# Message layer of a graph network: worked transposed, features spread over the partitions by fp32 matmuls

## The chip, the core and the metric

The program runs on one core of a Trainium2 chip. The metric is the device time of one execution in microseconds (us). The engines are TensorE (PE), VectorE (DVE), ScalarE (ACT), GpSimd (POOL) and the sync engine (SP); each works off its own list in order, and they wait for each other on semaphores. SBUF has 128 partitions; PSUM, where matmuls write, has eight banks of 512 fp32 a partition.

## The reference

Two message-passing layers on 12,500 nodes of 32 features and 200,000 edges, each followed by x = layernorm(x + aggregate). The edges come sorted by target node. Layer 0 takes the mean of the source features per target. Layer 1, the message layer, computes one 32-feature message per edge from the source's features, the edge's weight d and its direction r, and sums them per target:

```python
R = jax.nn.relu(d[:, None] @ w1 + b1) @ w2 + b2          # (E, 384)
Y = spherical_harmonics(rel_vec)                           # (E, 9)
Fj = features[src]                                         # (E, 32): 8 scalars, 8 vectors of 3
for i, (mo, lo) in enumerate(RS):                          # RS = [(8, 0), (8, 1)]
    for j, (mi, li) in enumerate(RS):
        for k, lf in enumerate(range(abs(lo - li), lo + li + 1)):
            acc += _NORM[i] * einsum('euv,ef,evi,ofi->euo', Rb[..., k], Yf, Fb, C)
```

The kernel rotates the vectors of an edge into a frame along r. There the message is, for every edge, a product of 384 radial values R with features and a sum over the 8 input channels v, for 32 outputs (8 scalars u and 3 components of 8 vectors u); then it rotates back.

## The kernel before, in words

Each partition holds 1564 consecutive edges, one edge per column. Columns are worked in batches of T = 16 (98 batches; the last has TL = 12), two batches k = 0, 1 per loop round. The message layer is the function layer1 of every engine. A batch there goes through these steps:

- POOL (lines 653-665): 16 indirect DMAs gather one source row of 32 features for each partition, one DMA per column, into got[k]; it may refill got[k] when rotated_in and f0_copied say that batch b-2 is read.
- SP (line 509): loads hid[k] (edge weights, copied to 64 partitions twice: even columns on partitions 0-63, odd ones on 64-127), the frames, and stores finished runs. It waits for radial_ready of an earlier batch.
- ACT (lines 786-809): relu turns the weights into the hidden layer; further the copies of the scalars (line 800), two of the turned components (803, 804), masks (700) and the turning of runs for the store (704).
- DVE (lines 1560-1605): rotation into the frame (1570 to 1581), then, for 6 groups of 3 or 2 columns (SIZES), two products of PSUM radial values with features (1592 and 1600) and a halving (1547) of the sum over v from 16 to 8 terms; in between turn_back (1534) of batch b-2 and its segmented scan (1350, 1355).
- PE (lines 966-992): radial(b, k, g) gives for each column of a group one bias matmul in bf16 (961) and one fp32 matmul (963), stationary hid (64 rows, 128 edges), moving wc (384 columns), into ps_r with edges on partitions. add_halves (934) sums the 8 remaining terms by 8 matmuls with the identity, add_axes (951) the three rotated-back components. PE's order is written out by hand in layer1; DVE's as well.

After the stage the node stage (L642, L1483 and on) gathers the sums of each node and normalises.

## Time and profile before

| | us |
|---|---|
| median of 3 runs | 3832.39 (3831.2 to 3833.62) |
| span of the profiled execution | 3826.4 |
| median less that span | 6.0 |
| PE busy | 3266.5 (85%) |
| DVE busy | 3211.4 (84%) |
| POOL busy | 2845.1 (74%) |
| ACT busy | 1391.8 (36%) |

The profile shows one execution; its own time is given as its span, from the first to the last instruction, and the runs' times are taken outside it. Busy times are shares of the whole span, with layer 0 in the first 1450 us and the message layer from about 1600 to 3690 us. A matmul in fp32 shows as two records. PEclk is the TensorE clock that was granted, as a share of 2.4 GHz.

### The profile page before, as it was taken

To read this page: it belongs to the slowest core of one execution; us is meant where nothing else is said; L and a number is where in the kernel's file an instruction comes from. 1 tells how busy PE (TensorE), PEld (TensorE's weight loads), DVE (VectorE), ACT (ScalarE), POOL (GpSimd) and SP (SyncE) were. 2 spreads that over 40 slices of the span, in tenths; PEclk is the share of its full clock that TensorE was granted. 3 is DMA by queue.
4 is the path that set the end of the run, shared out by engine and by line. 5 is a ranking of instruction groups with operands and counts; after the bars stand their busy time and mean duration, and the time that the engine had idled before them with its cause. 6 is when DMAs were issued, how large, how long until landed. Compare 5 with 4: busy or idle time off the path is not lost. (4 is left out here: it accounts for less than half of the span.)

```text
span 3826.4 us, 51167 instructions
## 1 busy us (share of the span) xinstructions
PE 3266.5 (85%) x14783; PEld 2108.0 (55%) x14783; DVE 3211.4 (84%) x4450; ACT 1391.8 (36%) x1803; POOL 2845.1 (74%) x2915
## 2 busy tenths in 40 slices
PE   4999999999999883288888988988989889889873
PEld 3898889898989773233333433333433334334342
DVE  5787877787878784589999999999999999999975
ACT  3777777776777650011111111111111111111110
POOL 7777777777777776677777777777777777777746
PEclk9999999999999995599999999999999999999985
DMA  4122222222222221122222222222222222222211
GB/s 99 39 56 41 54 40 43 52 45 50 44 52 41 50 51 27 37 54 54 61 52 57 56 61 52 60 52 60 53 61 51 61 51 61 52 61 55 58 33 25
DMA packets 188426, 197.62 MB, mean 52 GB/s; under 512 B 60241, under 2 KB 149427, under 8 KB 188085
## 3 DMA queue, kind: packets, MB, share of 16 engines
q1 hardware_dynamic: 95508, 149.13, 13.4%
q0 software_dynamic: 92832, 47.72, 10.1%
q14 instruction: 77, 0.63, 0.1%
q8 instruction: 9, 0.15, 0.0%
HBM read 134.02 MB, written 62.59 MB: 51 GB/s over the span
## 5 line engine op out<-in xcount | busy, mean ns | idle before, releaser
L663 POOL DMA_INDIRECT got<-x_d,idx x1564 | 1562.3, 999 | 510.0 <-issue 501.9
L963 PE MATMUL ps_r<-wc,hid 64*128 64x384 f32 x3128 | 791.4, 485 | 0.0
L886 PE MATMUL ps_r<-x_hi,hot_s 128*128 128x448 f32 x1974 | 742.7, 376 | 41.6 <-ACT hot_s L717 41.6
L886 PE MATMUL ps_r<-x_lo,hot_s 128*128 128x448 f32 x1974 | 733.5, 372 | 0.0
L704 ACT COPY runs_t<-runs 128x512 f32<-128x512 f32 x196 | 211.7, 1080 | 1098.8 <-DVE runs L1355 1098.7
L1592 DVE TENSOR_TENSOR prod<-ps_r,f_along 128x768 f32<-128x768 f32 (+1 forms) x586 | 503.3, 859 | 61.2 <-PE ps_r L963 31.4
L714 ACT ACTIVATE hot_s<-rows,minus_row 128x512 fp32r<-128x512 f16 (+1 forms) x658 | 448.9, 763 | 245.1 <-PE ps_m L886 204.7
L1600 DVE TENSOR_TENSOR prod<-ps_r,f_across 128x768 f32<-128x768 f32 (+1 forms) x586 | 504.2, 860 | 0.0
L963 PEld LDWEIGHTS ps_r<-wc,hid 64*128 64x128 f32 x3128 | 421.0, 190 | 106.7 <-issue 1.6
L934 PE MATMUL ps_m<-x_room,ident 128*128 128x512 f32 x768 | 409.6, 659 | 69.3 <-DVE x_room L1547 69.3
L934 PE MATMUL ps_m<-unit,ident 128*128 128x512 f32 x784 | 401.7, 637 | 48.6 <-DVE unit L1547 48.6
L886 PEld LDWEIGHTS ps_r<-x_hi,hot_s 128*128 128x128 f32 x1974 | 378.6, 192 | 75.8 <-issue 42.9
L886 PEld LDWEIGHTS ps_r<-x_lo,hot_s 128*128 128x128 f32 x1974 | 378.6, 192 | 33.0
L617 POOL DMA_INDIRECT got<-in_x_dram,idx_deep x322 | 312.3, 970 | 107.8 <-issue 43.2
L617 POOL DMA_INDIRECT f_across<-in_x_dram,idx_deep x331 | 314.7, 951 | 100.9 <-issue 43.0
L617 POOL DMA_INDIRECT f_along<-in_x_dram,idx_deep x326 | 315.4, 967 | 99.3 <-PE ps_r L886 40.2
L961 PE MATMUL ps_r<-bias_parts,ones_b 64*128 64x384 bf16 x1564 | 262.8, 332 | 132.7 <-DVE prod L1600 110.6
L886 PE MATMUL ps_m<-x_hi,hot_s 128*128 128x448 f32 x987 | 362.0, 367 | 0.0
L886 PE MATMUL ps_m<-x_lo,hot_s 128*128 128x448 f32 x987 | 361.5, 366 | 0.0
L961 PEld LDWEIGHTS ps_r<-bias_parts,ones_b 64*128 64x128 bf16 x1564 | 62.6, 93 | 526.5 <-DVE prod L1600 331.3
L717 ACT ACTIVATE hot_s<-hot_s 128x3584 fp32r<-128x3584 f32 x94 | 336.1, 3576 | 3.0
L934 PEld LDWEIGHTS ps_m<-x_room,ident 128*128 128x128 f32 x768 | 139.8, 202 | 283.0 <-issue 278.7
(202 smaller groups left out, 4427.9 us busy)
## 6 DMA issues: line engine op xcount, KB each, us to landing
hid<-weight_t SPq DMA_DIRECT2D x196, 256.0 KB
run_d<-runs_t SPq DMA_DIRECT2D x194, 256.0 KB
got<-x_d,idx POOLq DMA_INDIRECT x1564
rows<-code_d SPq DMA_DIRECT2D x47, 160.0 KB, 3.4
frame_d<-x_sb SPq DMA_DIRECT2D x7, 1008.0 KB, 4.5
frame<-frame_d SPq DMA_DIRECT2D x98, 72.0 KB
frame_b<-frame_d SPq DMA_DIRECT2D x98, 72.0 KB, 1.9
rows<-code_d SPq DMA_DIRECT2D x47, 128.0 KB
```

The costliest lines, as they stand in the source:

```text
L617: pool.indirect_dma_start(got_deep[k][:, t, :], None, x, bass.IndirectOffsetOnAxis(ap=idx_deep[q][:, k * T + t:k * T + t + 1], axis=0)).th ...
L663: pool.indirect_dma_start(got[k][:, t, :], None, x1_d, bass.IndirectOffsetOnAxis(ap=idx[k][:, t:t + 1], axis=0)).then_inc(got2_landed[k], 16)
L704: act.copy(runs_t[k][:, :, :], runs[k][:, :, :].rearrange("p f t -> p t f")).then_inc(done, 1)
L714: act.activation(hot_s[k][:, a, :, :], rows[k][:, :, :], ACT.Abs, bias=minus_row[:, a:a + 1]).then_inc(off_rows, 1)
L717: act.activation(hot_s[k][:, :, :, :], hot_s[k][:, :, :, :].bitcast(F32), ACT.Relu, bias=1.0, scale=-1.0).then_inc(hot_s_ready, 1)
L886: mm = pe.matmul(found[BANK_OF[k][g]], hot_s[k][:, a, g, :], part[:, a * LN * D:(a + 1) * LN * D], start=(a == 0 and n == 0), stop=(a == B ...
L934: mm = pe.matmul(terms2[k].rearrange("p o t -> p t o"), ident[:, :], halves[k][:, v, :, :], start=(v == 0), stop=(v == MUL - 1))
L961: pe.matmul(ps_r[:, g % 2, t, 0:RD], ones_b[rows, :], bias_parts[rows, :], start=True, stop=False)
L963: pe.matmul(ps_r[:, g % 2, t, 0:RD], hid[k][rows, c * P:(c + 1) * P], wc[rows, :], start=False, stop=True).then_inc(radial_ready, 1)
L1592: dve.tensor_tensor(prod[q][:, 0:size, 0:2, :, :], ps_r[:, q, 0:size, 0:256].rearrange("p t (b v u) -> p t b v u", b=2, u=MUL), spread(f_a ...
L1600: dve.tensor_tensor(prod[q][:, 0:size, 2:4, :, :], spread(ps_r[:, q, 0:size, 256:RD].rearrange("p t (v u) -> p t v u", u=MUL), 2, 2), spre ...
```

## The change

A batch is worked with (column, feature) on the partitions and edges along the free dimension.

- PE: `radial` now has wc stationary (128 of its 384 columns) and hid moving: a unit (c, h) gives 128 radial values for 4 x 128 edges of two columns-in-four, as two matmuls of 64 rows by 512 columns into the two banks of the one `radial_slot`. ACT copies each unit to SBUF and adds the bias there (`copy_radial`); the six bias matmul groups go. `turn_features` transposes the rotated features (4 transposes), ACT copies them to `ft`, and `spread_features` repeats them over 128 partitions by a matmul of 32 rows by 512 columns with a 0/1 matrix, two per unit, into two alternating slots of two banks.
- DVE: `multiply` makes 8 products of 2 x 512 elements per batch (SBUF times PSUM into SBUF). There is no halving.
- PE: `sum_products` sums over v by a matmul with a 0/1 matrix of 32 columns, 4 matmuls (one per column-in-four, each to 32 partitions of the one bank `summed_p`) for each of 4 blocks q. ACT copies the sums (`copy_summed`), `turn_messages` transposes them back (4 transposes), and from there turn_back, add_axes and the scan go as before, but for batch b-1 instead of b-2 and with one PSUM bank, so the scalars are copied out and added back by one more matmul.
- hot_p's room is used again for radial copies; the bias split in bf16 parts goes; a bias column and the 0/1 matrices are made at the start of the stage.

The core of the diff:

```diff
+            def copy_radial(b, u, w=QUAD * P):
+                c, h = RADIAL_UNITS[u]
+                act.wait_ge(radial_ready, UNITS * b + u + 1)
+                if not isinstance(b, int) or b > 0:
+                    act.wait_ge(multiplied, len(PRODUCTS) * (b - 1) + (1, 2, 3, 4, 7, 8)[u])
+                act.activation(radial_s[u][:, :, 0:w], radial_slot[:, :, 0:w], ACT.Identity,
+                               bias=bias_col[:, c:c + 1]).then_inc(radial_copied, 1)
+            def copy_summed(b, w=QUAD * P):
+                act.wait_ge(summed, BLOCKS * (b + 1))
+                if not isinstance(b, int) or b > 0:
+                    act.wait_ge(messages_ready, b)
+                act.copy(summed_t[:, 0:w], summed_p[:, 0:w]).then_inc(summed_copied, 1)
...
+                    first, final = isinstance(b, int) and b == 0, last and k == 1
+                    n = TL if final else T
+                    w = TL // QUAD * P if final else QUAD * P
+                    if not first:
+                        copy_summed(b - 1)
                     act.wait_ge(got2_landed[k], 16 * (T * i + n))
                     if not isinstance(b, int) or b > 1:
+                        act.wait_ge(turned, b - 1)
+                    act.copy(turned_in[k][:, 0:n, 0:MUL], got[k][:, 0:n, 0:MUL]).then_inc(f0_copied, 1)
+                    copy_radial(b, UNITS - 1, w)
                     act.copy(idx[k][:, :], src_all[:, bass.ds((b + 2) * T, T)]).then_inc(idx_ready, 1)
+                    act.wait_ge(turned, b + 1)
+                    if not first:
+                        act.wait_ge(spread_ready, UNITS * b)
+                    act.copy(ft[:, 0:w], spread_slot[k][:, 0, 0:w]).then_inc(ft_ready, 1)
+                    if not first:
+                        masks2(b - 1, 1 - k)
+                    if not final:
+                        later = TL // QUAD * P if last else QUAD * P
+                        for u in range(4):
+                            copy_radial(b + 1, u, later)
+                    if not first:
+                        carry_and_turn(b - 1, 1 - k)
+                    if not last:
+                        relu(k, i + 2)
+                    if not final:
+                        copy_radial(b + 1, 4, later)
...
+            def radial(b, k, u, w=QUAD * P):
+                c, h = RADIAL_UNITS[u]
+                if u == 0:
+                    pe.wait_ge(hid_ready, b + 1)
+                if not isinstance(b, int) or UNITS * b + u > 0:
+                    pe.wait_ge(radial_copied, UNITS * b + u)
+                for t in range(2):
+                    half = slice(t * H, (t + 1) * H)
+                    mm = pe.matmul(radial_slot[:, t, 0:w], wc[half, c * P:(c + 1) * P],
+                                   hid[k][half, :].rearrange("p (j c e) -> p j c e", c=2, e=P)[:, 0:w // P, h, :],
+                                   start=True, stop=True)
+                mm.then_inc(radial_ready, 1)
+            def turn_features(b, k, w=QUAD * P):
+                pe.wait_ge(rotated_in, b + 1)
+                pe.wait_ge(f0_copied, b + 1)
+                if not isinstance(b, int) or b > 0:
+                    pe.wait_ge(multiplied, len(PRODUCTS) * b - 1)
+                for j in range(w // P):
+                    mm = pe.transpose(spread_slot[k][:, 0, j * P:(j + 1) * P],
+                                      turned_in[k][:, QUAD * j:QUAD * (j + 1), :].rearrange("p t f -> p (t f)"), ident[:, :])
+                mm.then_inc(turned, 1)
+            def spread_features(b, k, s, w=QUAD * P):
+                c, h = SPREADS[s]
+                slot = spread_slot[(k + s + 1) % 2]
+                if s == 0:
+                    pe.wait_ge(ft_ready, b + 1)
+                    if not isinstance(b, int) or b > 0:
+                        pe.wait_ge(multiplied, len(PRODUCTS) * b)
+                if s > 1:
+                    pe.wait_ge(multiplied, len(PRODUCTS) * b + (2, 4, 5, 6)[s - 2])
+                for t in range(2):
+                    group = slice((2 * h + t) * D, (2 * h + t + 1) * D)
+                    mm = pe.matmul(slot[:, t, 0:w], repeat[group, c, :], ft[group, 0:w], start=True, stop=True)
+                mm.then_inc(spread_ready, 1)
+            def sum_products(b, q, w=QUAD * P):
+                pe.wait_ge(multiplied, len(PRODUCTS) * b + (3, 4, 6, 8)[q])
+                if q == 0 and (not isinstance(b, int) or b > 0):
+                    pe.wait_ge(summed_copied, b)
+                for t in range(QUAD):
+                    mm = pe.matmul(summed_p[t * D:(t + 1) * D, 0:w], to_feature[:, D - MUL - q * MUL:2 * D - MUL - q * MUL],
+                                   product[q][t // 2][:, t % 2, 0:w], start=(q == 0), stop=(q == BLOCKS - 1))
+                mm.then_inc(summed, 1)
+            def turn_messages(b, w=QUAD * P):
+                pe.wait_ge(summed_copied, b + 1)
+                if not isinstance(b, int) or b > 0:
+                    pe.wait_ge(scanned, BATCHES + b)
+                for j in range(w // P):
+                    mm = pe.transpose(ps_m[:, 0, j * P:(j + 1) * P], summed_t[:, j * P:(j + 1) * P], ident[:, :])
+                mm.then_inc(messages_ready, 1)
...
             def layer1(i, last=False):
                 for k in range(2):
                     b = 2 * i + k
+                    first, final = isinstance(b, int) and b == 0, last and k == 1
+                    short = TL // QUAD * P
+                    w = short if final else QUAD * P
+                    later = short if last else QUAD * P
+                    if not first:
+                        sum_products(b - 1, 3)
+                        turn_messages(b - 1)
+                    turn_features(b, k, w)
+                    if not final:
+                        radial(b + 1, 1 - k, 0, later)
+                    spread_features(b, k, 0, w)
+                    spread_features(b, k, 1, w)
+                    if not first:
+                        add_axes(b - 1)
+                    if not final:
+                        radial(b + 1, 1 - k, 1, later)
+                    spread_features(b, k, 2, w)
+                    sum_products(b, 0, w)
+                    sum_products(b, 1, w)
+                    if not final:
+                        radial(b + 1, 1 - k, 2, later)
+                    spread_features(b, k, 3, w)
+                    if not final:
+                        radial(b + 1, 1 - k, 3, later)
+                    spread_features(b, k, 4, w)
+                    if not final:
+                        radial(b + 1, 1 - k, 4, later)
+                    spread_features(b, k, 5, w)
+                    sum_products(b, 2, w)
+                    if not final:
+                        radial(b + 1, 1 - k, 5, later)
...
+            def multiply(b, k, n, w):
+                q, h = PRODUCTS[n]
+                u = RADIAL_UNITS.index((min(q, 2), h))
+                s_ = SPREADS.index((max(q - 1, 0), h))
+                dve.wait_ge(radial_copied, UNITS * b + u + 1)
+                dve.wait_ge(spread_ready, UNITS * b + s_ + 1)
+                if h == 0 and (not isinstance(b, int) or b > 0):
+                    dve.wait_ge(summed, BLOCKS * (b - 1) + q + 1)
+                dve.tensor_tensor(product[q][h][:, :, 0:w], radial_s[u][:, :, 0:w], spread_slot[(k + s_ + 1) % 2][:, :, 0:w],
+                                  ALU.mult).then_inc(multiplied, 1)
             def layer1(i, first, last=False):
                 for k in range(2):
                     b = 2 * i + k
                     short = last and k == 1
                     n = TL if short else T
+                    w = n // QUAD * P
                     dve.wait_ge(got2_landed[k], 16 * (T * i + n))
                     dve.wait_ge(frame_loaded[k], 16 * (i + 1))
...
                     for c in range(3):
                         s.mark(dve.tensor_tensor(part[:, c, 0:n], spread(f1[:, :, :, c], 2, 3),
                                                  spread(frame[k][:, 0:n, c, :], 3, MUL), ALU.mult))
+                    s.settle()
+                    s.mark(dve.tensor_tensor(part[:, 0, 0:n], part[:, 0, 0:n], part[:, 1, 0:n], ALU.add))
+                    s.settle()
+                    if not isinstance(b, int) or b > 1:
+                        dve.wait_ge(turned, b - 1)
+                    dve.tensor_tensor(turned_in[k][:, 0:n, MUL:D], part[:, 0, 0:n].rearrange("p t i v -> p t (i v)"),
+                                      part[:, 2, 0:n].rearrange("p t i v -> p t (i v)"), ALU.add).then_inc(rotated_in, 1)
                     if not (first and k == 0):
+                        turn_back(b - 1, 1 - k)
+                    for m in range(4):
+                        multiply(b, k, m, w)
+                    if not (first and k == 0):
+                        scan2(b - 1, 1 - k)
+                    for m in range(4, len(PRODUCTS)):
+                        multiply(b, k, m, w)
```

## Rows read from the trace of the kernel before

**Rows 1.** Stretches: stretch, length; busy us of PE, PEld, DVE, ACT, POOL; PEclk, DMA, GB/s
```profile
1700.00:3600.00 1900.00, 1700.35 (x6285) 751.42 (x6285) 1789.19 (x2605) 330.41 (x626) 1436.10 (x1438) 0.97 0.25 57
```
**Rows 2.** The page: granted TensorE clock in 40 equal slices of the span
```profile
PEclk9999999999999995599999999999999999999985
```
**Rows 3.** Instructions of line 1570: durations, first and last start
```profile
L1570 DVE TENSOR_TENSOR part<-got,frame x294: 532/665/687, 1615.3 to 3665.9; 128x384 f32<-128x384 f32 x146, 128x288 f32<-128x288 f32 x1
```
**Rows 4.** Groups by line, shapes apart, 1700 to 3600 us
```profile
L663 POOL DMA_INDIRECT got<-x_d,idx x1438 | 1436.8, 999 | 464.1 <-issue 464.1
L963 PE MATMUL ps_r<-wc,hid 64*128 64x384 f32 x2871 | 722.7, 482 | 0.0
L934 PE MATMUL ps_m<-x_room,ident 128*128 128x512 f32 x720 | 384.2, 659 | 65.6 <-DVE x_room L1547 65.6
...
L1592 DVE TENSOR_TENSOR prod<-ps_r,f_along 128x768 f32<-128x768 f32 x360 | 342.3, 951 | 55.0 <-DVE f_across L1581 27.2 <-PE ps_r L963 26.5
...
L951 PE MATMUL ps_m<-back,ident 128*128 128x384 f32 x540 | 190.2, 489 | 0.0
...
L1570 DVE TENSOR_TENSOR part<-got,frame 128x384 f32<-128x384 f32 x270 | 164.7, 665 | 49.7 <-DMA got<-x_d,idx 49.0
L1534 DVE TENSOR_TENSOR back<-ps_m,frame_b 128x384 f32<-128x384 f32 x270 | 133.7, 554 | 0.0
...
L788 ACT ACTIVATE hid<-hid,b_col,w_col 128x1024 f32<-128x1024 f32 x90 | 110.3, 1225 | 0.0
...
L704 ACT COPY runs_t<-runs 128x512 f32<-128x512 f32 x89 | 96.7, 1086 | 899.5 <-DVE runs L1355 899.5
...
L700 ACT COPY masks<-same 128x480 f32 x89 | 52.6, 591 | 0.0
L1577 DVE TENSOR_TENSOR part<-part 128x384 f32<-128x384 f32 x90 | 49.8, 553 | 0.0
```
**Rows 5.** Waits, 1700 to 3600 us: who for whom, us, times, longest
```profile
ACT f_along L800 <- DMA got<-x_d,idx: 144.7, 57, 6.1
...
DVE part L1570 <- DMA got<-x_d,idx: 49.0, 24, 3.8
```
**Rows 6.** Instructions of line 663, 1700 to 3600 us
```profile
L663 POOL DMA_INDIRECT got<-x_d,idx x1438: 940/944/1692, 1700.1 to 3599.7; - x180
```
**Rows 7.** Timeline of DVE: start, length, instruction
```profile
3000.85 0.95 DVE L1592 TENSOR_TENSOR prod<-ps_r,f_along 128x768 f32<-128x768 f32 x1
3001.72 0.95 DVE L1547 TENSOR_TENSOR x_room<-prod 128x768 f32<-128x768 f32 x1
...
3012.13 0.68 DVE L1592 TENSOR_TENSOR prod<-ps_r,f_along 128x512 f32<-128x512 f32 x1
3012.73 0.68 DVE L1547 TENSOR_TENSOR x_room<-prod 128x512 f32<-128x512 f32 x1
```
**Rows 8.** Timeline of PE, one batch (a matmul in fp32 is two records)
```profile
3002.71 1.12 PE L934 MATMUL ps_m<-unit,ident 128*128 128x512 f32 x2
...
3005.48 1.98 PE L934 MATMUL ps_m<-unit,ident 128*128 128x512 f32 x4
...
3006.88 0.59 PE L934 MATMUL ps_m<-unit,ident 128*128 128x512 f32 x1
...
3007.57 0.81 PE L963 MATMUL ps_r<-wc,hid 64*128 64x384 f32 x4
3008.31 0.70 PE L934 MATMUL ps_m<-unit,ident 128*128 128x512 f32 x1
```
**Rows 9.** Instructions of line 859, fp32 transposes of layer 0
```profile
L859 PE MATMUL ps_r<-ident,prod_room x4: 421/421/477, 41.4 to 42.1; 128*128 128x128 f32 x3, 128*39 128x128 f32 x1
```
**Rows 10.** Timeline of DVE, end of the message layer
```profile
3681.53 0.95 DVE L1600 TENSOR_TENSOR prod<-ps_r,f_across 128x768 f32<-128x768 f32 x1
...
3690.07 1.22 DVE L1355 TENSOR_TENSOR_SCAN runs<-masks,ps_m 128x512 f32<-128x512 f32 x1
```
**Rows 11.** Timelines of PE and ACT, start of the message layer
```profile
1601.38 0.80 PE L961 MATMUL ps_r<-bias_parts,ones_b 64*128 64x384 bf16 x3 [18.30 <-DVE bias_parts L1266]
...
1615.31 0.40 ACT L800 COPY f_along<-got 128x256 f32<-128x256 f32 x1 [15.56 <-DMA got<-x_d,idx]
```

More of the change, by code:

```diff
@@ L28 @@
 NPP = 98
-SG = 3
-SIZES = (3, 3, 3, 3, 2, 2)
-GROUPS = len(SIZES)
-FIRST = [sum(SIZES[:g]) for g in range(GROUPS)]
+QUAD = 4
+HALVES = 2
+BLOCKS = 4
+RADIAL_UNITS = ((0, 0), (1, 0), (0, 1), (1, 1), (2, 0), (2, 1))
+PRODUCTS = ((0, 0), (1, 0), (0, 1), (1, 1), (2, 0), (2, 1), (3, 0), (3, 1))
+SPREADS = ((0, 0), (0, 1), (1, 0), (1, 1), (2, 0), (2, 1))
+UNITS = len(RADIAL_UNITS)
 NC = 7
@@ L673, in _ @@
             pool.wait_ge(ngot_used[0], CHUNKS)
-            pool.wait_ge(radial_ready, T * (BATCHES - 1) + TL)
+            pool.wait_ge(radial_ready, UNITS * BATCHES)
             pool.sem_inc(pool_go, 1)
@@ L803, in layer1 @@
-                    act.copy(f_across[k][:, 0:n, 1, 0, :], f_across[k][:, 0:n, 0, 1, :]).then_inc(turned_copied, 1)
-                    act.activation(f_across[k][:, 0:n, 1, 1, :], f_across[k][:, 0:n, 0, 0, :], ACT.Copy,
-                                   scale=-1.0).then_inc(turned_copied, 1)
-                    if not (last and k == 1):
-                        relu(1 - k, i + 1 + k)
-                    if not isinstance(b, int) or b > 1:
-                        carry_and_turn(b - 2, k)
+                    act.wait_ge(turned, b + 1)
@@ L953, in add_axes @@
-                mm.then_inc(axes_summed, 1)
-            def radial(b, k, g):
-                if not isinstance(b, int) or b > 0 or g > 1:
-                    pe.wait_ge(multiplied, GROUPS * b + g - 1)
-                tiles = [((FIRST[g] + t) // 2, slice((FIRST[g] + t) % 2 * H, (FIRST[g] + t) % 2 * H + H))
-                         for t in range(SIZES[g])]
-                for t, (c, rows) in enumerate(tiles):
-                    pe.matmul(ps_r[:, g % 2, t, 0:RD], ones_b[rows, :], bias_parts[rows, :], start=True, stop=False)
-                for t, (c, rows) in enumerate(tiles):
-                    pe.matmul(ps_r[:, g % 2, t, 0:RD], hid[k][rows, c * P:(c + 1) * P], wc[rows, :],
-                              start=False, stop=True).then_inc(radial_ready, 1)
+                    pe.matmul(terms2[:, MUL:D, :].rearrange("p (u i) t -> p t i u", i=3)[:, 0:n], ident[:, :],
+                              back[:, a, 0:n], start=(a == 0), stop=(a == 2), skip_group_check=True)
@@ L997, in _ @@
+            pe.wait_ge(wc_ready, 1)
+            pe.wait_ge(bias_made, 1)
+            for c in range(3):
+                mm = pe.transpose(turned_bias[:, c * P:(c + 1) * P], bias_rooms[1][:, c * P:(c + 1) * P], ident[:, :])
+            mm.then_inc(bias_turned, 1)
+            for u in range(UNITS):
+                radial(0, 0, u)
+            pe.wait_ge(bias_ready, 1)
+            pe.wait_ge(spreads_made, 1)
             layer1(0)
@@ L1241, in make_wc, with make_constants @@
                                                 ALU.mult, ALU.add)
-            def make_bias_parts():
-                b2_all, bias, left, part_f = bias_rooms
-                for n in range(3):
-                    s.mark(dve.tensor_scalar(part_row[:, n:n + 1], node[:, 0:1], float(NPP * n), None, ALU.is_equal))
-                s.mark(dve.memset(ones_b[:, :], 1.0))
+            def make_constants():
+                b2_all, bias = bias_rooms
                 dve.wait_ge(loaded_b2, 16)
+                last = make_wc(b2_all, bias)
+                last.then_inc(bias_made, 1)
+                s.mark(dve.memset(to_feature[:, :], 0.0))
+                s.mark(dve.tensor_reduce(in_group[:, :], ident[:, :].rearrange("p (t f) -> p f t", f=D), AX.X, ALU.add))
@@ L1250, in make_bias_parts @@
                 s.settle()
-                for n in range(3):
-                    s.mark(dve.scalar_tensor_tensor(part_row[:, n:n + 1], node[:, 0:1], float(NPP * (H + n)),
-                                                    part_row[:, n:n + 1], ALU.is_equal, ALU.add))
-                s.mark(make_wc(b2_all, bias))
-                s.settle()
-                s.mark(dve.tensor_copy(bias_parts[:, :], bias))
-                s.settle()
-                s.mark(dve.tensor_tensor(left, bias, bias_parts[:, :], ALU.subtract))
@@ L1571, in layer1 @@
                                                  spread(frame[k][:, 0:n, c, :], 3, MUL), ALU.mult))
-                    if not (first and k == 0):
-                        halve(b - 1, 1 - k, GROUPS - 1)
-                    if not first:
-                        turn_back(b - 2, k)
                     s.settle()
@@ L1607, in _ @@
+                    if not (first and k == 0):
+                        scan2(b - 1, 1 - k)
+                    for m in range(4, len(PRODUCTS)):
+                        multiply(b, k, m, w)
             loop(layer1, PAIRS - 1, 2)
             layer1(PAIRS - 1, False, True)
-            halve(BATCHES - 1, 1, GROUPS_L - 1)
-            turn_back(BATCHES - 2, 0)
-            turn_back(BATCHES - 1, 1, part, False, TL)
-            for b in (BATCHES - 2, BATCHES - 1):
-                scan2(b, b % 2)
+            turn_back(BATCHES - 1, 1, TL)
```

193 lines of the change are left out of this document (66 added, 127 removed).

## The prediction, written before the changed kernel was run

> **What bounds the kernel now.** I read the table of stretches first. From 1700 to 3600 us the message layer runs in steady state: DVE is busy for 1789 of 1900 us, PE for 1700, ACT for only 330, at a granted clock of 0.97 of 2.4 GHz [rows 1]. The gaps in that clock are short: the slices show 9 nearly everywhere but at the two node stages [rows 2]. The first and last start of line 1570, three per batch, give the length of a batch: (3665.9 - 1615.3) / 97 = 21.1 us [rows 3]. Anything saved or lost per batch counts 98 times.
>
> By that table DVE looks like the bound. The groups by line show a second one. POOL issues one gather per column: 1438 of them, 1436.8 us busy and 464.1 us between them, which is 1.32 us each and 1901 us of 1900 [rows 4]. Sixteen make 21.1 us, exactly the batch. The idle time is all "issue", the fixed 0.3 us that follows each gather; POOL waits for almost nobody. The other side of it is in the waits: DVE's line 1570 waited 49.0 us and ACT's line 800 144.7 us for gathered rows [rows 5]. So two engines are at their limit together, and POOL is untouched by the change. Its gathers take 0.944 us at the median, 0.94 at least and 1.69 at most [rows 6]; if all took 0.94 a batch would still need 16 x (0.94 + 0.305) = 19.9 us. **No relief of DVE can bring more than 21.1 - 19.9 = 1.2 us per batch, 118 us in all**; what gathers lose beyond 0.944 us has to go too for that.
>
> **The change part by part.** Per batch of 16 columns, with durations from the steady state.
>
> *DVE.* Removed are 12 products and 6 halvings. One 768-element operation starts 0.87 us after the other (3000.85, 3001.72), one of 512 elements 0.60 us (3012.13, 3012.73) [rows 7]. There are 12 of the large and 6 of the small: 14.0 us. Added are 8 products of 1024 elements. The two rows lie on a line of 0.27 us per 256 elements, so 1.14 us each, 9.1 us. Line 1579 and 1581 together become one 384-element operation (0.55 us as line 1577 [rows 4]); a 128-element copy ahead of turn_back adds about 0.2. DVE's own sum, with busy time of a line over 90 batches: parts 164.7/90 = 1.8, add 0.6, rotated 0.55, copy 0.2, turn_back 133.7/90 = 1.5, products 9.1, carry and scan 1.5 [rows 4]: **15.2 us**. It stops being a bound.
>
> *ACT.* Added: 6 bias copies of 1024 elements out of PSUM, 1 of 512 for the sums, 1 of 512 for the turned features. Line 788 does 1024 elements in 1.225 us, line 700 480 in 0.59 [rows 4]. A copy from PSUM has no row at this size; between as fast as line 788 and half as much again. I take line 788's. New ACT sum: 6 x 1.2 + 2 x 0.65 + masks 0.6 + turned runs 1.1 + ReLU 1.2 + small ones 0.4 = 11.8 us. It fits, but in written order: the copies of radial unit 4 stand behind turned runs and the ReLU.
>
> *PE.* Removed: 16 bias matmuls in bf16, 16 of 384 columns, 8 sums of halves of 512 columns. Added: 12 radial and 12 spreading matmuls of 512 columns, 16 summing ones of 512 columns by 32, 8 transposes, and one 128-column matmul beside the axes. An fp32 matmul of 512 columns shows as two records; between two of them line 934 goes on at 0.86 us (1.98 us for four records, 1.12 for two [rows 8]). What 40 such matmuls cost depends on how many run side by side: one after another they are 34 us. For row halves the trace answers: the four records of line 963 at 3007.57 are two matmuls on partitions 0-63 and 64-127, each record 0.48 us long, and all end 0.81 us later [rows 8]; one alone would take 0.86 x 384/512 = 0.64 and a tail of about 0.17. So **two row groups in different banks run wholly side by side**: a pair of 512 columns costs 0.86 us. The radial pairs are of this kind; the spreading pairs are on 32 rows instead of 64, and I take the same. 12 pairs: 10.3 us (20.6 if nothing overlapped).
>
> The 16 summing matmuls use all 128 rows and four different column groups, all in one bank. **No row before shows column groups.** Side by side, four cost 0.86 us and a batch 3.4 us; in sequence 13.7 us; in twos 6.9. I take 3.4, since row groups overlap fully, and keep the others as cases. The Trainium skill, "TensorE: Matmul & The Clock Gate", Part 3, reports a speed-up of 2.38 for three column tiles of 512 columns; as an estimate from that ratio, a three-tile group costs 3/2.38 = 1.26 of one matmul, so a sum of four about 1.1 us instead of 0.86. The total by that page would be near 3990 us, by full overlap 3890, and no run here shows it yet.
>
> Axes: three full-height matmuls of 384 columns, as now, are 3 x 0.86 x 384/512 = 1.9, and the one of 128 columns 0.2. Transposes: four lines 859 start within 0.7 us, 0.23 each, near the start of the kernel [rows 9]; half that if only the clock differs. 8 x 0.16 = 1.3 us.
>
> A change of shape has a price as well. After the pair at 3007.57 the next full-height matmul starts at 3008.31, 0.74 us later instead of 0.64, and then takes 0.70 us where its neighbours take 0.59 [rows 8]: 0.2 us, its weights not loaded ahead. The new order of PE changes shape 16 times a batch (now 8 times). That is 3.2 us, or 1.6 where weights of 32 columns load fast.
>
> PE's sum: 10.3 + 3.4 + 2.1 + 1.3 + 3.2 = **20.3 us** (18.7 with the cheap shape changes, 19.4 if the first two spreads, on four row groups, overlap). Now it is 1700 / 90 = 18.9.
>
> *New waits on PE.* PE takes its waits in written order, and two of them cover nothing. First, after the last sum of a batch it waits for ACT's copy of the sums before it can turn the messages: tail 0.17, copy 0.65, two handoffs of 0.05 = 0.9 us. Behind it are queued turn_features and everything DVE needs for its next product. Second, radial results have a single slot; unit u+1 waits until ACT has copied unit u: 0.17 + 1.2 + 0.1 = 1.5 us after its end, of which a spreading pair and a shape change hide 1.1. That leaves about 0.4 us three times when the copies are prompt. The last of them (unit 5) waits for the copy of unit 4, and that waits for DVE's seventh product. But the DVE products need the spreads only just made, so part of these waits run while DVE catches up and the summing matmuls would have waited too. I take 0.9 + 0.6 = 1.5 us. **PE's round: 21.8 us**; bounds 20.3 (waits covered, cheap shapes) to 22.8.
>
> *What moves.* SP's reload of hid waits for radial_ready of batch b-1, which now comes a batch earlier; POOL's gathers still wait for rotated_in and f0_copied, both early in a batch. hid is reloaded before it is needed: a round is left for it. A batch is finished one round earlier (b-1 instead of b-2), which changes only the end. There the last product at 3681.53 and the last scan at 3690.07 [rows 10] are 8.5 us apart; new: sum 0.8, copy 0.65, transposes 0.7, turn_back 1.4, axes 1.6, carry and scan 1.5, handoffs 0.4 = 7 us: -1.5. In front, PE starts at 1601.38 and ACT's first copy of gathered features at 1615.31 [rows 11]; six radial units with copies at 2.4 us each fit in these 14 us. Then the first product comes some 3 us later. Together +1 us, nothing.
>
> *Sum.* 21.8 - 21.1 = +0.7 us x 98 = +69 us. With small change at start and end the span goes from 3826.4 to about 3896. The median of the runs shown, 3832.4, lies 6.0 above that span; rounding down for the overlap that the first two spreads may have, I say **3890 us**.
>
> **The rivals.**
> 1. *Column groups run one after another.* For it: no row shows them, and all four stream 128 rows at once, unlike the row halves. Against it: the row halves overlap without any loss. Price: sums 13.7 instead of 3.4, 10.3 us per batch, of which the waits absorb about 0.9: 31.2 us, +10.1 x 98 = +990, **4820 us**.
> 2. *They overlap only partly* (two at a time, or slowed by the shared bank). Sums 5 to 7 us: round 23.5 to 25.3, **4060 to 4240 us**.
> 3. *The gathers bind and PE fits under them: faster.* Place: PE's round. Price and turning point: shape changes at 0.1 us and all waits covered give 18.7 + 0.9 = 19.6, under POOL's 21.1; it decides below 21.0. If the gathers stretch less beside a DVE with 6 us of rest, the batch falls to 20.0-20.9: -0.2 to -1.1 us, **3725 to 3813 us**. For it: gathers of 0.944 us are the median and the stretched ones come in bursts. Against: the 256 KB loads of hid per half, which stay, run in the same bursts.
> 4. *The same with gathers as slow as now:* the batch stays 21.1, **3832 us**.
>
> **How the numbers follow.** Forecast (round 21.3 to 23.2, 3845 to 4040): 0.39. Rival 1: 0.14. Rival 2: 0.14. Rival 3: 0.25. Rival 4: 0.08. A measurement of this kernel tells 0.2%, 8 us, from no change. Faster 0.25, same 0.08, slower 0.67. The forecast's own range is 3845 to 4040; the range for 8 in 10 has to take in rivals 3 and 2, so 3750 to 4350, leaving out rival 1 and the best twentieth of rival 3.
>
> **What would show it.** DVE busy per batch near 15 us, with idle time ended by spreads. Pairs on 32 rows: four records within about 1.05 us. The summing matmuls: eight records within about 1.1 us if side by side, 3.5 if not; this one group tells forecast from rival 1. PE busy over 90% of the stage and POOL no longer 100%: idle behind rotated_in. If POOL still is at 16 x 1.32 us with no waits, the forecast was wrong and rivals 3 or 4 hold. ACT copies of 1024 from PSUM much above 1.3 us would move the bound to the chain through the single radial slot.

## The result, and the profile after

The changed kernel takes 3801.41 us (3798.03 to 3805.39) against 3833.01: a ratio of 0.9921, 95% interval 0.9909 to 0.9932. It is 0.8% faster, 32 us. The forecast was 3890 and slower.

The stretches of the changed kernel, columns as in [rows 1]; first the node stage and the start, then the steady state of the message layer:

```profile
1460.00:1580.00 120.00, 43.57 (x192) 41.71 (x192) 59.67 (x148) 3.89 (x13) 89.78 (x96) 0.50 0.13 25
1580.00:1700.00 120.00, 90.73 (x393) 28.30 (x393) 67.93 (x113) 49.05 (x59) 85.34 (x90) 0.81 0.26 55
1700.00:3600.00 1900.00, 1757.98 (x8736) 574.99 (x8732) 1398.01 (x1729) 958.67 (x1183) 1408.43 (x1463) 1.00 0.26 57
```

Beside [rows 1], DVE fell from 1789 to 1398 us, ACT rose from 330 to 959, PE from 1700 to 1758, and the clock granted to PE is 1.00, where it was 0.97. The gathers are 1463 instead of 1438 in the same time: 1.7% more. The groups by line, which answer to [rows 4]:

```profile
L688 POOL DMA_INDIRECT got<-x_d,idx x1463 | 1409.3, 963 | 491.9 <-issue 474.8 <-ACT f_along L842 17.1
L990 PE MATMUL ps_r<-hid,wc 64*128 64x512 f32 x2184 | 616.4, 641 | 67.4 <-ACT prod_room L822 62.5 <-issue 4.8
L1018 PE MATMUL ps_r<-ft,repeat 32*128 32x512 f32 x2184 | 514.0, 640 | 0.0
L1645 DVE TENSOR_TENSOR x_room<-radial_more,ps_r 128x1024 f32<-128x1024 f32 x364 | 442.1, 1215 | 358.0 <-PE ps_r L1018 240.7 <-ACT prod_room L822 117.3
...
L822 ACT ACTIVATE prod_room<-ps_r,bias_col 128x1024 f32<-128x1024 f32 x364 | 405.6, 1114 | 722.7 <-PE ps_r L990 498.0 <-DVE unit L1645 224.8
...
L1027 PE MATMUL ps_m<-x_room,to_feature 128*32 128x512 f32 x1456 | 193.9, 605 | 0.0
...
L1659 DVE TENSOR_TENSOR part<-got,frame 128x384 f32<-128x384 f32 x273 | 169.6, 677 | 0.0
```

Three readings. DVE now waits for PE's spreads and ACT's copies. The gathers were 0.999 us at the mean and are 0.963, with 0.32 us between them as before (464.1/1438 and 474.8/1463, "issue" alone): sixteen of them with these gaps make 21.1 us before and 20.6 after. And DVE's line 1659 (1570 before) no longer waits for gathered rows: the 49.0 us of [rows 5] are gone. POOL even waits a little for others (17.1 us for ACT). So POOL doesn't seem to be the bound any more; experiment 3 tests it.

One round of PE, from the first two spreads of a batch to those of the next (start, length, instruction; in brackets idle time before it):

```profile
2999.84 1.14 PE L1018 MATMUL ps_r<-ft,repeat 32*128 32x512 f32 x8
3000.91 2.20 PE L1043 MATMUL ps_m<-back,ident 128*128 128x384 f32 x6
3002.95 0.39 PE L1045 MATMUL ps_m<-f_across,ident 128*128 128x128 f32 x2
3003.61 1.13 PE L990 MATMUL ps_r<-hid,wc 64*128 64x512 f32 x4 [0.27 <-ACT prod_room L822]
3004.67 1.13 PE L1018 MATMUL ps_r<-ft,repeat 32*128 32x512 f32 x4
3005.72 1.92 PE L1027 MATMUL ps_m<-unit,to_feature 128*32 128x512 f32 x16
3007.58 1.13 PE L990 MATMUL ps_r<-hid,wc 64*128 64x512 f32 x4
3008.64 1.13 PE L1018 MATMUL ps_r<-ft,repeat 32*128 32x512 f32 x4
3010.00 1.13 PE L990 MATMUL ps_r<-hid,wc 64*128 64x512 f32 x4 [0.24 <-ACT prod_room L822]
3011.06 1.13 PE L1018 MATMUL ps_r<-ft,repeat 32*128 32x512 f32 x4
3012.42 1.13 PE L990 MATMUL ps_r<-hid,wc 64*128 64x512 f32 x4 [0.23 <-ACT prod_room L822]
3013.48 1.13 PE L1018 MATMUL ps_r<-ft,repeat 32*128 32x512 f32 x4
3014.54 1.07 PE L1027 MATMUL ps_m<-x_room,to_feature 128*32 128x512 f32 x8
3015.53 1.13 PE L990 MATMUL ps_r<-hid,wc 64*128 64x512 f32 x4
3016.59 1.07 PE L1027 MATMUL ps_m<-x_room,to_feature 128*32 128x512 f32 x8
3018.44 0.65 PE L1037 MATMUL ps_m<-ident,f_across 128*128 128x128 f32 x4 [0.78 <-ACT f_across L829]
3019.05 0.65 PE L1002 MATMUL ps_r<-ident,f_along 128*128 128x128 f32 x4
3019.63 1.13 PE L990 MATMUL ps_r<-hid,wc 64*128 64x512 f32 x4
3020.68 1.14 PE L1018 MATMUL ps_r<-ft,repeat 32*128 32x512 f32 x8
```

PE's round (the time that one batch takes it) is 3020.68 - 2999.84 = 20.84 us. Four waits make 0.27 + 0.24 + 0.23 + 0.78 = 1.52 us of it. A pair of 512 columns with its change of shape is 1.06 us. Four summing matmuls on four column groups (eight records) take 1.07 us. And the first two spreads, four matmuls on four row groups, also take 1.14 us together.

### The profile page after: what moved, and what is told of

Same layout as the page of the kernel before. It is cut to its first block, busy times and chain, and to the rows that moved or that the text cites. A ratio compares the mean times of both kernels' runs of the same rounds, so it can differ in the third digit from the quotient of the medians.

```text
span 3796.3 us, 58108 instructions
## 1 busy us (share of the span) xinstructions
PE 3310.6 (87%) x17312; PEld 1902.1 (50%) x17312; DVE 2762.8 (73%) x3470; ACT 2061.5 (54%) x2391; POOL 2786.3 (73%) x2915
## 4 chain that ended last, share of the span: by engine, by line
PE 70%; ACT 12%; DVE 5%; POOL 5%; issue 5%; DMA 1%; SPq 0%; ACTq 0%; DVEq 0%; POOLq 0%
PE ps_r L940 19%; PE ps_r L990 17%; PE ps_m L1027 10%; PE ps_m L940 10%; PE ps_r L1018 8%; ACT prod_room L822 8%; POOL ngot L667 4%; DVE unit L1645 3%; PE ps_m L1037 2%; PE ps_r L1002 2%; ACT f_across L829 2%; PE ps_r L924 1%; ACT hot_s L739 1%; PE ps_m L1043 1%; ACT hot_s L742 1%
## 5 line engine op out<-in xcount | busy, mean ns | idle before, releaser
L688 POOL DMA_INDIRECT got<-x_d,idx x1564 | 1506.2, 963 | 530.6 <-issue 504.7
L822 ACT ACTIVATE prod_room<-ps_r,bias_col 128x1024 f32<-128x1024 f32 x392 | 435.9, 1112 | 780.0 <-PE ps_r L990 531.9
L1645 DVE TENSOR_TENSOR x_room<-radial_more,ps_r 128x1024 f32<-128x1024 f32 x392 | 475.0, 1212 | 384.0 <-PE ps_r L1018 252.3
L990 PE MATMUL ps_r<-hid,wc 64*128 64x512 f32 (+1 forms) x2352 | 669.8, 646 | 81.2 <-ACT prod_room L822 72.9
L1018 PE MATMUL ps_r<-ft,repeat 32*128 32x512 f32 (+1 forms) x2352 | 553.4, 639 | 1.1 <-ACT ft L848 0.6
L1645 DVE TENSOR_TENSOR unit<-prod_room,ps_r 128x1024 f32<-128x1024 f32 x392 | 451.1, 1213 | 106.9 <-PE ps_r L1018 102.0
L990 PEld LDWEIGHTS ps_r<-hid,wc 64*128 64x128 f32 x2352 | 178.8, 186 | 448.8 <-ACT prod_room L822 255.3
L1018 PEld LDWEIGHTS ps_r<-ft,repeat 32*128 32x128 f32 x2352 | 148.0, 183 | 371.0 <-issue 150.3
L667 POOL DMA_INDIRECT ngot<-run_d,pos x196 | 185.0, 944 | 111.5 <-issue 59.1
L1369 DVE TENSOR_TENSOR prod_room<-ps_r,hot_l 128x448 f32<-128x448 f32 x282 | 167.6, 620 | 118.8 <-PE ps_r L940 109.9
```

Of the source, the lines that this page charges most:

```text
L667: pool.indirect_dma_start(ngot[c][:, j, :], None, table, bass.IndirectOffsetOnAxis(ap=pos[:, node_j:node_j + 1], axis=0)).then_inc(ngot_la ...
L688: pool.indirect_dma_start(got[k][:, t, :], None, x1_d, bass.IndirectOffsetOnAxis(ap=idx[k][:, t:t + 1], axis=0)).then_inc(got2_landed[k], 16)
L822: act.activation(radial_s[u][:, :, 0:w], radial_slot[:, :, 0:w], ACT.Identity, bias=bias_col[:, c:c + 1]).then_inc(radial_copied, 1)
L990: mm = pe.matmul(radial_slot[:, t, 0:w], wc[half, c * P:(c + 1) * P], hid[k][half, :].rearrange("p (j c e) -> p j c e", c=2, e=P)[:, 0:w / ...
L1018: mm = pe.matmul(slot[:, t, 0:w], repeat[group, c, :], ft[group, 0:w], start=True, stop=True)
L1645: dve.tensor_tensor(product[q][h][:, :, 0:w], radial_s[u][:, :, 0:w], spread_slot[(k + s_ + 1) % 2][:, :, 0:w], ALU.mult).then_inc(multipl ...
```

## The experiments

The kernel before ran on the same chip beside each of these runs, at medians of 3829 to 3831 us, and ratios are against it. The changed kernel didn't run again: where a total is set against its 3801.41 us, differences of some 4 us mean nothing. Several of the kernels leave work out or work on wrong data, which is said; they are for timing alone.

**1. Are the first two spreads really side by side, and does PE's round set the time?** The second spread reads the row groups of the first, so its products get the features of other columns.

```diff
-                    group = slice((2 * h + t) * D, (2 * h + t + 1) * D)
+                    g = t if s == 1 else 2 * h + t
+                    group = slice(g * D, (g + 1) * D)
```

> The changed kernel, but the second spread of a batch reads the same two row groups (partitions 0-63) as the first; its products get the features of other columns, nothing else differs. Theory A (PE's written order sets the batch, and the first two spreads run side by side on four row groups): the two spreads take 1.9 us instead of 1.07, the batch 20.83 + 0.85 = 21.7 us, the total 3801 + 83 = about 3885 us. Theory B (the gathers on POOL set the batch and PE has room): POOL's 16 x 1.27 = 20.3 us stay below, the total moves by less than 20 us.

Measured: 3851.04 us (3850.82 to 3854.09), ratio 1.0054 (1.0037 to 1.0071). PE in its steady state:

```profile
3014.18 1.99 PE L1019 MATMUL ps_r<-ft,repeat 32*128 32x512 f32 x8
3016.09 2.20 PE L1044 MATMUL ps_m<-back,ident 128*128 128x384 f32 x6
3018.13 0.39 PE L1046 MATMUL ps_m<-f_across,ident 128*128 128x128 f32 x2
3018.45 1.13 PE L990 MATMUL ps_r<-hid,wc 64*128 64x512 f32 x4
```

The two spreads take 1.99 us instead of 1.14, the 0.85 expected. The total rose by 50 us, 0.51 per batch, not by 83. The last row shows why: the wait of 0.27 us ahead of this radial unit is gone. Work added in front of a wait is paid only beyond it. The total came out 34 us under the 3885 expected. Theory A holds in kind; its price was too high by what the wait absorbs (0.27 of the 0.34 us per batch that are missing; the rest wasn't looked into).

**2. Do column groups run side by side?** Each summing matmul gets 128 stationary columns; the widening of the 0/1 matrix that goes with it is not shown.

```diff
-                    mm = pe.matmul(summed_p[t * D:(t + 1) * D, 0:w], to_feature[:, D - MUL - q * MUL:2 * D - MUL - q * MUL],
-                                   product[q][t // 2][:, t % 2, 0:w], start=(q == 0), stop=(q == BLOCKS - 1))
+                    mm = pe.matmul(summed_p[:, 0:w], to_feature[:, P - MUL - t * D - q * MUL:2 * P - MUL - t * D - q * MUL],
+                                   product[q][t // 2][:, t % 2, 0:w], start=(q == 0 and t == 0),
+                                   stop=(q == BLOCKS - 1 and t == QUAD - 1))
```

> The changed kernel, but each summing matmul has 128 stationary columns (zeros outside its 8) and adds into all 128 partitions, so that there are no column groups; the result is the same. Theory A (column groups run side by side, and without them four matmuls take 4 x 0.86 us): sums cost 13.7 instead of 3.4 us per batch, less some 0.5 us of waits and shape changes that go, so the batch is 30.6 us, the total about 3801 + 98 x 9.8 = 4760 us. Theory B (the side-by-side look of the records is only their model, and the sums are in series already): no change, 3801 us.

Measured: 4817.28 us (4815.58 to 4818.3), ratio 1.2576 (1.2555 to 1.2597): 10.4 us more per batch. The sixteen records of line 1027 that took 1.92 us:

```profile
3006.49 7.13 PE L1027 MATMUL ps_m<-unit,to_feature 128*128 128x512 f32 x16
```

Theory A in kind, though the batch rose by 10.4 us and not by the 9.8 expected (4760 us). This is also the kernel of rival 1 of the prediction, which gave 4820. That it is so near is in part luck: rival 1 started from a round of 21.8 us, which is 0.96 too long, and took off 0.9 us for waits that would absorb a part; nothing like that was absorbed. In the changed kernel, four matmuls on four column groups into one bank show no extra cost: a second group of four adds 1.92 - 1.07 = 0.85 us.

**3 and 4. Which engine bounded the kernel before, and which after?** Both kernels with 12 gathers per batch instead of 16; the other four columns keep old rows. The waits of ACT and DVE for gathered rows count accordingly:

```diff
+GT2 = 12
...
-                    for t in range(TL if last and k == 1 else T):
+                    for t in range(GT2 if rounds > 0 else T):
...
-                    act.wait_ge(got2_landed[k], 16 * (T * i + n))
+                    act.wait_ge(got2_landed[k], 16 * (T + GT2 * i))
```

> The changed kernel, but from the third batch of the message layer on only 12 of the 16 columns are gathered; the other four keep old rows. Theory A (PE binds): 3801 us within 10 us, at best less by what a late gather costs now and then. Theory B (POOL's gathers bind): the batch falls by what they lack, 0.5 us or more, to 3750 us or below.

> The kernel before, with the same cut of the gathers to 12 per batch. Theory A (before, gathers at 1.32 us each set the batch of 21.1 us and DVE alone could do it in 20.25 us, the length of an undisturbed batch in the trace): the total falls by 98 x 0.85 = 83 us to about 3750 us. Theory B (DVE bound it, and the change gained by relieving DVE): 3833 us within 10 us.

Measured: after with 12 gathers 3801.34 us (3796.41 to 3805.9), unchanged; before with 12 gathers 3741.05 us (3740.45 to 3741.7), ratio 0.9767 (0.975 to 0.9783), 90 us less. The gathers of experiment 3 (line 689, 1700 to 3600 us) and then of experiment 4 (line 664, 1700 to 3500 us):

```profile
L689 POOL DMA_INDIRECT got<-x_d,idx x1092 | 1030.4, 944 | 870.4 <-ACT idx L845 558.9 <-issue 311.5
```

```profile
L664 POOL DMA_INDIRECT got<-x_d,idx x1068 | 1064.5, 997 | 735.5 <-issue 735.5
```

So before, the gathers set the batch, and DVE's own round was 21.1 - 90/98 = 20.2 us: with 12 gathers DVE is busy for 1767 of the 1800 us. After, relief of POOL is worth nothing, and experiment 1 showed that added work on PE costs time: PE sets the batch. The rows hold a surprise: a quarter of the gathers is gone in both, but one takes 0.944 us in the first and still 0.997 in the second.

**5. What is next behind PE?** The summing matmuls of blocks 1 and 2 are left out, and with them their share of the messages.

```diff
-                pe.wait_ge(multiplied, len(PRODUCTS) * b + (3, 4, 6, 8)[q])
+                pe.wait_ge(multiplied, len(PRODUCTS) * b + (4, 4, 6, 8)[q])
...
-                mm.then_inc(summed, 1)
+                mm.then_inc(summed, 2)
...
-                    sum_products(b, 1, w)
...
-                    sum_products(b, 2, w)
```

> The changed kernel without the summing matmuls of blocks q = 1 and q = 2 (their share of the messages is left out); PE's batch gets 1.9 us shorter on paper. Theory A (behind PE at 20.83 us the gathers are next, 16 x (0.963 + 0.305) = 20.3 us): the batch stops at 20.3 to 20.4 us, the total near 3755 us. Theory B (nothing but PE is near): 3801 - 98 x 1.5 = 3655 us, a part of the gain being lost in waits for ACT's copies.

Measured: 3759.89 us (3759.65 to 3760.97), ratio 0.9817 (0.9802 to 0.9832). The batch is 20.84 - 41.5/98 = 20.4 us; its gathers are 0.960 us and 0.32 apart, 20.5 for sixteen. Theory A: the gathers stand close behind PE, by 0.4 us in the total of this run, and by 0.2 us in the changed kernel's own rows (20.6 against 20.84).

**6 and 7. PE's longest wait.** In 6 DVE issues line 1659's three products ahead, between its products of the batch before. They become a function `make_part`, and are gone from the start of the batch; shown is where they are issued:

```diff
                     for m in range(4, len(PRODUCTS)):
+                        if m > 4 and not short:
+                            make_part(i + k, 1 - k, m - 5, TL if last else T)
                         multiply(b, k, m, w)
```

In 7, with that, PE and ACT change their order. PE's part is shown; ACT copies `ft` ahead of radial unit 5, and the sums after the indices:

```diff
                         sum_products(b - 1, 3)
-                        turn_messages(b - 1)
                     turn_features(b, k, w)
-                    if not final:
-                        radial(b + 1, 1 - k, 0, later)
+                    if not first:
+                        turn_messages(b - 1)
                     spread_features(b, k, 0, w)
                     spread_features(b, k, 1, w)
+                    if not final:
+                        radial(b + 1, 1 - k, 0, later)
```

> The changed kernel with one edit on DVE: the three rotation products of batch b+1 are issued between the last four products of batch b, where DVE stands idle for 1.1 to 1.5 us each time, instead of after them. Theory A (PE's order and its wait for the copied sums set the batch, and turn_features stands behind turn_messages): no change, 3801 us within 10. Theory B (the rotation on DVE is late and holds PE): the batch gets up to 0.6 us shorter, to about 3745 us.

> As e6, and PE turns the features before it turns the messages, so that this covers its wait of 0.78 us for the copied sums; ACT copies the turned features ahead of radial unit 5, and PE's first radial unit comes after the first two spreads. Theory A (that wait is a real cost of PE's round): PE could do 19.9 us, and the gathers at 16 x 1.27 = 20.3 us take over: total 3801 - 98 x 0.5 = about 3750 us, faster than both kernels. Theory B (another chain, through DVE's turn_back or ACT's single radial slot, is as long): less than 15 us gained.

Measured: 6 gave 3799.31 us (3796.93 to 3800.62), no change, as theory A. But 7 gave 3817.83 (3810.86 to 3822.45), ratio 0.9966 (0.9952 to 0.9979): 16 us slower than the changed kernel, where both theories had it no slower. Excerpts of DVE and POOL of it, where the gathers stretch (the products of line 1646 stand between the DVE rows):

```profile
3002.57 0.67 DVE L1655 TENSOR_TENSOR part<-got,frame 128x384 f32<-128x384 f32 x1 [3.26 <-DMA got<-x_d,idx]
...
3004.28 0.67 DVE L1655 TENSOR_TENSOR part<-got,frame 128x384 f32<-128x384 f32 x1
...
3005.99 0.70 DVE L1655 TENSOR_TENSOR part<-got,frame 128x384 f32<-128x384 f32 x1
...
3007.74 0.55 DVE L1666 TENSOR_TENSOR part<-part 128x384 f32<-128x384 f32 x1
```

```profile
3001.41 0.95 POOL L688 DMA_INDIRECT got<-x_d,idx  x1 [0.30 <-issue]
3002.66 1.38 POOL L688 DMA_INDIRECT got<-x_d,idx  x1 [0.30 <-issue]
3004.34 1.40 POOL L688 DMA_INDIRECT got<-x_d,idx  x1 [0.30 <-issue]
3006.05 1.42 POOL L688 DMA_INDIRECT got<-x_d,idx  x1 [0.30 <-issue]
3007.78 1.33 POOL L688 DMA_INDIRECT got<-x_d,idx  x1 [0.30 <-issue]
3009.41 0.94 POOL L688 DMA_INDIRECT got<-x_d,idx  x1 [0.30 <-issue]
```

Each stretched gather begins while a DVE operation runs whose two inputs are in SBUF. The products of line 1646 in between, with one input in PSUM, stretch none: in the whole steady state 589 gathers began beside one, at 0.944 us in the mean. The first DVE row shows that DVE was waiting for gathered rows again: 7 is bound by gathers, at 0.994 us each, which experiment 8 confirms.

**8. Was PE's round shortened all the same?** As 7, with 12 gathers per batch; the other columns keep old rows.

> As e7, with only 12 of 16 columns gathered from the third batch on (the others keep old rows). Theory A (in e7 the gathers bind at 20.3 us, PE's own round is 19.9 us): about 3715 us, some 35 us under e7. Theory B (e7 is bound by PE or by a chain through ACT or DVE): the same as e7 within 8 us.

Measured: 3707.65 us (3705.65 to 3708.5), ratio 0.968 (0.9665 to 0.9695). PE's round is 20.84 - 93.8/98 = 19.9 us, as worked out. Theory A; the gain is there and the gathers hide it.

**9. The three products in one block**, to touch fewer gathers; the edit is shown against 7:

```diff
-                        if m > 4 and not short:
-                            make_part(i + k, 1 - k, m - 5, TL if last else T)
+                        if m == 6 and not short:
+                            for c in range(3):
+                                make_part(i + k, 1 - k, c, TL if last else T)
```

> As e7 (3818 us, gathers at 0.994 us), but the three rotation products stand in one block ahead of the seventh product instead of singly ahead of the sixth, seventh and eighth. In e7 four gathers in a row took 1.33 to 1.42 us, each beside one of the five spaced DVE operations with two SBUF operands. Theory A (each such operation can hold up one gather, so a block holds up fewer): stretched gathers fall from 2.25 to about 1.5 per batch, the batch from 21.0 to 20.6 us, the total to about 3785 us. Theory B (what counts is only how many such operations there are): as e7, 3818 us.

Measured: 3782.26 us (3780.55 to 3783.74), ratio 0.9874 (0.9858 to 0.9891), the fastest version with the whole work, 19 us under the changed kernel. Gathers:

```profile
L688 POOL DMA_INDIRECT got<-x_d,idx x1469 | 1431.9, 975 | 469.0 <-issue 466.0 <-ACT idx L841 2.1 <-DVE f_along L1670 0.9
```

0.975 + 0.319 = 1.29 us, 20.7 for sixteen: the batch is still POOL's. Theory A: 137 gathers over 1.05 us in 1700 to 3600 us, 1.5 per batch, against 202 and 2.2 in 7, with the same 286 and 287 us of DVE operations on two SBUF inputs.

**10 and 11. Do two SBUF inputs stretch a gather?** Four idle-time products of 512 elements added to the changed kernel, in 10 with the line as shown, in 11 with `ps_m[:, 0, 0:w]` as the second input:

```diff
+                        if m in (5, 6):
+                            for e in range(2):
+                                dve.tensor_tensor(spare_room[:, (2 * (m - 5) + e) * 512:(2 * (m - 5) + e) * 512 + w],
+                                                  radial_s[4][:, 0, 0:w], radial_s[4][:, 1, 0:w], ALU.mult)
```

> The changed kernel with four added DVE products of 512 elements per batch, in the idle time ahead of the sixth and seventh product (two each, 1.2 us, against gaps of 1.5 and 1.3 us); both inputs and the output lie in SBUF, the output is not used. Theory A (a DVE operation with both inputs in SBUF holds up the gathers on POOL): gathers rise from 0.963 us to 1.0 us or more, POOL's batch to 20.9 to 21.3 us, the total to 3815 to 3845 us. Theory B (the stretch has to do with other work at that place, such as the reading of fresh rows): gathers stay at 0.963 us, total 3801 within 10.

> As e10 with one difference: the second input of the four added products is a PSUM bank that is idle then. Theory A (only two SBUF inputs hold up the gathers): gathers 0.963 us, total 3801 within 10. Theory B (any DVE work does, by its share of time): the same rise as e10.

Measured: 10 gave 3818.35 us (3814.8 to 3820.13), ratio 0.9973 (0.9961 to 0.9984); 11 gave 3801.62 (3799.57 to 3805.35), ratio 0.993 (0.9913 to 0.9946), as without the addition. Added products and gathers of 10, then of 11:

```profile
L688 POOL DMA_INDIRECT got<-x_d,idx x1443 | 1439.7, 998 | 461.2 <-issue 457.5 <-ACT f_along L842 3.0 <-ACT idx L844 0.6
...
L1677 DVE TENSOR_TENSOR spare_room<-radial_more 128x512 f32<-128x512 f32 x360 | 231.3, 683 | 0.0
```

```profile
L688 POOL DMA_INDIRECT got<-x_d,idx x1466 | 1412.8, 964 | 489.6 <-issue 472.9 <-ACT f_along L842 16.8
...
L1677 DVE TENSOR_TENSOR spare_room<-radial_more,ps_m 128x512 f32<-128x512 f32 x364 | 232.3, 679 | 0.0
```

The same DVE time, 231 and 232 us. With two SBUF inputs the gathers go from 0.963 to 0.998 us and the total up by 17 us; with one of them in PSUM neither moves. Theory A.

The trace of the kernel before shows the same, gather by gather. Here are a product and a halving of DVE, and two gathers; the halving that the second gather meets, at 3012.73, is in [rows 7]:

```profile
3010.08 0.67 DVE L1592 TENSOR_TENSOR prod<-ps_r,f_along 128x512 f32<-128x512 f32 x1
3010.66 0.95 DVE L1547 TENSOR_TENSOR x_room<-prod 128x768 f32<-128x768 f32 x1
```

```profile
3010.39 0.94 POOL L663 DMA_INDIRECT got<-x_d,idx  x1 [0.30 <-issue]
3012.88 1.34 POOL L663 DMA_INDIRECT got<-x_d,idx  x1 [0.30 <-issue]
```

The first gather begins beside a product that reads PSUM and keeps its 0.94 us, though a halving starts 0.27 us later. The second begins 0.15 us into a halving and ends 0.81 us after it. Over 1700 to 3600 us the 1438 gathers lose 79 us beyond 0.944 each. By the DVE operation that was running as they began, 42 us go to halvings, 30 to line 1570, 7 to line 1581, all with two SBUF inputs; the 682 gathers that began beside a product from PSUM average 0.944 us.

This agrees with a rule of the Trainium skill, "SBUF — State Buffer", section "Who interferes with whom": a DVE operation with two SBUF inputs contends with GpSimd's reads of SBUF, and one with at most one such input does not. The same section of the Trainium skill infers that such a `tensor_tensor` leaves the generation of DMA descriptors alone; here it does hold up the indirect gathers, and the measurement decides.

## Why the prediction was wrong

*What bounds before.* Right: experiment 4 shows the gathers at 21.1 us a batch and DVE at 20.2 behind them. With that the largest possible gain was small, and it was.

*"POOL is untouched by the change."* Wrong, and one of the two steps that failed. The halvings (line 1547, 4.7 us per batch) read two SBUF tiles; the new product reads SBUF and PSUM. With them went 42 of the 79 us by which gathers were stretched, and 28 are left. The mean fell from 0.999 to 0.963 us, and POOL's batch from 21.1 to 16 x (0.963 + 0.325) = 20.6. I had written of this only as a chance in rival 3, as "rest" for DVE. It wasn't rest: experiment 11 gives DVE the same load as 10 and the gathers don't notice. I put the bursts of slow gathers down to the loads of hid; between 10 and 11 those loads are the same and only the place of one DVE operand differs. The floor of 19.9 us was too low as well: it takes 0.305 us between gathers, while [rows 4] have 464.1/1438 = 0.323 at the mean, which makes 20.2.

*PE's round.* Said 21.8, measured 20.84. Its parts:

| term | said | measured |
|---|---|---|
| row pair of 512 columns with its shape change | 0.86 + 0.2 | 1.06 |
| first two spreads | 1.72 | 1.07 with the step to the next |
| summing group of four | 0.86 + change | 1.0 |
| 8 transposes | 1.3 | 1.2 |
| waits | 0.9 + 0.6 | 0.78 + 0.74 |

The mis-sized term is the one of the two spreads, and this is the other step that failed: I took no overlap between them for the central value and named it only as a bound (19.4 instead of 20.3), though they lie on four different row groups and [rows 8] showed that two row groups overlap fully. The runs showed four side by side, 1.07 us for both (experiment 1: 1.99 us without it). That is 0.86 of the 0.96 us, and enough to turn "slower" into "no slower", because the forecast was only 0.7 us above the old batch. It is not enough for "faster": a PE round of 20.9 us under gathers that still take 21.1 is rival 4, 3832 us. For the 32 us that were gained both had to fail, the spreads on PE and POOL's "untouched".

*Column groups.* Right at 3.4 us per batch, without a row for them: four times 0.85, besides the changes of shape. The ratio of 2.38 that the Trainium skill has for three column tiles ("TensorE: Matmul & The Clock Gate", Part 3), from which the prediction estimated 1.1 us for a group of four, isn't borne out here: eight records end within 1.07 us with their tail, and a further group adds 0.85.

*Waits on PE.* Right in place and size (1.5 us). Experiments 1 and 8 show how they count: one absorbed 0.27 of an added 0.85 us, and covering the long one brought the round to 19.9.

*DVE and ACT.* DVE said 15.2 us, measured 1398 / 91 = 15.4. ACT's copy from PSUM said 1.2, measured 1.11. Neither binds, as said.

*The outcome* is rival 3's kind, faster with PE under 21.0, with this difference: the gathers fell below PE, and PE at 20.84 binds. Its range was 3725 to 3813; that 3801 lies in it doesn't make its mechanism right. (Its 19.6 us also adds the wait of 0.9 us that it calls covered.)

*Ends of the stage.* They were taken at nothing, and are worth 8.5 us. From the first and last start of line 1659 (1612.5 and 3641.5 us) the batch is 20.92 us in the mean, against 21.14: 22 of the 30.1 us by which the span is shorter. The others are outside: the first rotation starts 2.8 us earlier, and from the last rotation to the last scan it is 5.7 us less (18.5 against 24.2 us). The mean holds a loss as well: the first batch took 25.2 us, where 20.9 is the median. PE's granted clock was 0.55 from 1596 to 1629 us, and a radial pair took 2.08 us there against 1.13 later.

## What to carry to other kernels

When two engines are at their limit together, a change that relieves one is bounded by the other, and the first test is to cut the other's work; that test, here twelve gathers instead of sixteen, costs a few lines. Look also at which operands of a busy DVE operation lie in SBUF: two SBUF inputs beside a stream of indirect gathers lengthen the gathers, so moving one input to PSUM can speed up POOL without a change on it. And if a forecast hangs on 0.7 us of a 21 us round, an overlap that the rows bear out belongs in the central value, not in the bounds.

## What the runs showed of the hardware

- Four fp32 matmuls on four row groups into four banks, or on four column groups into one bank, take the time of one: 1.14 and 1.07 us for eight records of 512 columns, against 1.12 for one such matmul in [rows 8], 1.99 for two pairs after each other (experiment 1) and 7.13 / 2 = 3.6 us at full width (experiment 2).
- A gather of one row per partition takes 0.944 us alone. If it begins while a DVE operation with two SBUF inputs runs, it can be stretched: to 1.05 to 1.47 us in the changed kernel, to 1.69 at most before. Every gather over 1.05 us, in the kernel before, the changed one and the eight experiments that have more than two such gathers, ended 0.78 to 0.83 us after the end of the DVE operation that was running as it began. With 12 gathers placed where there were none of these operations (experiment 3), the longest was 0.961 us.
- A stretched gather so waits for one such operation, even where the next follows at once. That is why spreading them out is worse than keeping them together: 0.994 against 0.975 us (experiments 7 and 9), 36 us in all. What in a gather's first tenths of a microsecond has to wait isn't shown by any run.
